# Second layer of a graph network: the running count of edges in one place of a PSUM bank, and a new order on VectorE

## The reference

```python
x = _layernorm(x + _L0_gnn_ref(x, node_vec, edge_weight, edge_attr_64, edge_index, ...))   # attention
x = _layernorm(x + _L1_gnn_ref(x, src, dst, edge_weight, W, b))

def _L1_gnn_ref(x, rows, cols, vals, W, b):        # rows = src, cols = dst
    gathered = vals[:, None] * x[cols]
    agg = jax.ops.segment_sum(gathered, rows, num_segments=N_NODES)
    return jnp.einsum('nc,oc->no', agg, W) + b
```

## Time and profile before

| what | value |
|---|---|
| median of 3 runs | 9,845.34 us (9,844.81 to 9,847.26) |
| profiled execution, its own time | 9,864.48 us |
| its span, first to last instruction | 9,862.8 us |
| mean granted PE clock over the span | 0.822 |
| busy share of the span | PE 77%, DVE 87%, ACT 52%, POOL 68% |
| second layer, first scan to end | 5,225.0 to 9,862.8 us |

### The profile page before, as it was taken

The page is one execution under the profiler, slowest core; times in us unless marked ns, Lnnn a source line. Parts: engine busy times, 40 slices in busy tenths (PEclk is TensorE's granted clock), DMA queues, the critical chain, the costliest instruction groups (busy, mean ns, idle before and its releaser), DMA issues.

```text
span 9862.8 us, 272152 instructions
## 1 busy us (share of the span) xinstructions
PE 7624.6 (77%) x52868; PEld 7101.3 (72%) x52869; DVE 8560.3 (87%) x21301; ACT 5115.0 (52%) x20838; POOL 6708.6 (68%) x6871
## 2 busy tenths in 40 slices
PE   6477777777777777777756777788888888888855
PEld 2477777777777777777756777787888877877754
DVE  5899999999999999999987666799999999999968
ACT  2377777777777777777753333333333333333300
POOL 0477777777777777777745777777777777777720
PEclk8688988888888888898875555688888888888888
DMA  6467666676666666666632222355555555555544
GB/s 191 114 180 178 179 177 177 178 179 178 176 177 180 177 176 177 178 181 177 177 97 69 71 71 71 106 151 147 149 147 149 148 148 149 148 148 149 148 133 116
DMA packets 1631706, 1484.67 MB, mean 151 GB/s; under 512 B 792007, under 2 KB 1363043, under 8 KB 1631203
## 3 DMA queue, kind: packets, MB, share of 16 engines
q1 hardware_dynamic: 1374244, 848.34, 34.3%
q0 software_dynamic: 257088, 632.95, 22.8%
HBM read 1225.51 MB, written 254.87 MB: 150 GB/s over the span
## 4 chain that ended last, share of the span: by engine, by line
issue 25%; DVE 19%; POOL 18%; PE 14%; DMA 7%; ACT 7%; DVEq 6%; SPq 3%; ACTq 2%; POOLq 0%
POOL message_scratch L869 17%; DMA message_scratch<-ohT,idx 6%; PE bank L982 3%; DVE y_all L1537 3%; PE bank L973 3%; ACT arena L1154 2%; DVEq L531 2%; PE bank L955 2%; PE bank L1015 2%; PE bank L963 2%; DVE acc L1670 1%; SPq L728 1%; DVE oh L1583 1%; DVE oh L1576 1%; DVE kve L1523 1%
## 5 line engine op out<-in xcount | busy, mean ns | idle before, releaser
L817 POOL DMA_INDIRECT kv<-kv_scratch,arena x3136 | 3265.7, 1041 | 1236.6 <-issue 837.5
L869 POOL DMA_INDIRECT message_scratch<-ohT,idx x3232 | 3214.2, 994 | 1079.0 <-issue 880.2
L1261 ACT ACTIVATE ohT<-bank,kv 128x128 f32<-128x128 f32 x3232 | 923.9, 369 | 2703.8 <-DMA message_scratch<-ohT,idx 2665.1
L1154 ACT ACTIVATE arena<-arena,weights 128x65 f32<-128x65 f32 x7040 | 1771.6, 337 | 2.4 <-PE bank L982 2.3
L1063 PE MATMUL bank<-acc,oh 128*128 x6464 | 1211.2, 345 | 520.3 <-ACT ohT L1262 514.4
L1063 PEld LDWEIGHTS bank<-acc,oh 128*128 128x128 f32 x6464 | 1054.7, 247 | 627.7 <-issue 625.2
L1077 PE MATMUL bank<-oh,kve 128*128 128x128 f32 x8640 | 1387.7, 321 | 144.7 <-DVE arena L1838 107.8
L982 PE MATMUL bank<-arena,oh 128*128 128x130 f32 x7040 | 1164.1, 318 | 280.8 <-DVE acc L1670 274.8
L1077 PEld LDWEIGHTS bank<-oh,kve 128*128 128x128 f32 x8640 | 1248.0, 227 | 167.8 <-issue 157.3
L982 PEld LDWEIGHTS bank<-arena,oh 128*128 128x128 f32 x7040 | 1048.2, 227 | 362.6 <-issue 295.1
L973 PE MATMUL bank<-arena,ohT 128*128 128x128 f32 x7040 | 1090.6, 306 | 0.0
(11 more groups left out here) (232 smaller groups left out, 12653.6 us busy)
## 6 DMA issues: line engine op xcount, KB each, us to landing
kve<-message_scratch SPq DMA_DIRECT2D x2160, 129.0 KB
kve<-nodes_scratch SPq DMA_DIRECT2D x880, 256.0 KB
feat<-in_edge_attr_dram SPq DMA_DIRECT2D x880, 96.0 KB
feat<-block_scratch SPq DMA_DIRECT2D x812, 98.0 KB
arena<-q_scratch SPq DMA_DIRECT2D x880, 64.0 KB
message_scratch<-ohT,idx POOLq DMA_INDIRECT x3232
kv<-kv_scratch,arena POOLq DMA_INDIRECT x3136
feat<-in_edge_attr_dram SPq DMA_DIRECT2D x880, 32.0 KB
```

Source lines behind the costliest of these rows:

```text
L817: pool.indirect_dma_start(kv[:, k, g, :], None, kv_d, bass.IndirectOffsetOnAxis(ap=group_rows[:, half, k * G + g, 0:1].bitcast(I32), axis= ...
L869: pool.indirect_dma_start(msg_d, bass.IndirectOffsetOnAxis(ap=idx[:, k, g:g + 1], axis=0), sum_ring[:, k % RING1, g, :], None).then_inc(s_ ...
L1154: op = act.activation(wv[:, st.k % 2, g, h, :], vR[:, st.k, g, h, :], ACT.Copy, scale=weights[:, st.k // ROUND, g, st.k % ROUND, h:h + 1])
L1261: act.activation(sum_ring[:, st.k % RING1, g, 0:C], banks[2 + st.k % 2][:, g * P:(g + 1) * P], ACT.Copy, scale=taken[:, st.k, g, 2:3])
```

## The change

The ranks move from two buffers in SBUF to one place in bank 0, 98 partitions of 512 numbers. The scan of a step then overwrites the ranks of the step before, so the product of the step before (found_stage) must come first: it moves from behind the row numbers to ahead of the first segment addition, and the scan waits for it. The carry and the scan move behind the first segment addition and the row numbers, and the copy of ranks (posw_stage) behind the scan.

```diff
--- before.py
+++ after.py
@@ -234,7 +234,6 @@
         seg_oh = oh_all[:, RING1 * G * P:RING1 * G * P + SEG_OH * SEGMENT * 2 * P].rearrange("p (h b a n) -> p h b a n", h=SEG_OH, b=SEGMENT, a=2)
         assert MT == 4 * SEGMENT and UNROLL1 % (MT // SEGMENT) == 0
         blk_row = feat_flat[:, RING1 * 2 * P:RING1 * 2 * P + KS * G * P // 2].bitcast(BF16).rearrange("p (k e) -> p k e", k=KS)
-        ranks = prod
         found1 = [featT_all[:, 0, :], featT_all[:, 1, :], feat_flat[:, 0:G * P], feat_flat[:, G * P:2 * G * P]]
         zeros = oh_all[:, QS * G * P * 2 - (CHUNK * NCHUNKS - COLS) * 4:QS * G * P * 2]
         W7 = FB * C
@@ -303,6 +302,7 @@
         featT_ps = banks[1][0:TD + MSG, :]
         e_ps, q_ps = banks[2:4], banks[4:6]
         agg_ps = [banks[6 + j][:, 0:HEADS * HB] for j in range(2)]
+        ranks = banks[0][0:NB, :]
         irow_ps, one_ps = banks[7][:, 0:P], banks[7][0:NB, P:P + 1]
         RANKS = SEGMENT * P
         mT_ps, small_ps = banks[0][:, 0:G * ROWS], banks[0][:, 128:128 + 4 * ROWS]
@@ -1754,26 +1754,26 @@
 
                 if st.k == 0 and not (isinstance(st.i, int) and st.i == 0):
                     dve.wait_ge(s_carry, st.s + st.i - 1)
-                    dve.tensor_tensor(carry[0:NB, :], ranks[0:NB, 1, G * P - 1:G * P], jump[0:NB, bass.ds(st.i, 1)], ALU.add).then_inc(s_carry, 1)
+                    dve.tensor_tensor(carry[0:NB, :], ranks[:, G * P - 1:G * P], jump[0:NB, bass.ds(st.i, 1)], ALU.add).then_inc(s_carry, 1)
 
             def count_stage(st):
 
                 dve.wait_ge(s_inblk, st.s + 1)
-                wait(dve, s_pos, st.before(2))
+                wait(dve, s_pos, st.s)
                 first = isinstance(st.i, int) and st.i == 0
                 if st.k == 0:
                     since = jump[0:NB, 0:1] if first else carry[0:NB, :]
                 else:
-                    since = ranks[0:NB, (st.k + 1) % 2, G * P - 1:G * P]
+                    since = ranks[:, G * P - 1:G * P]
                 wait(dve, s_carry, st.s + st.i)
-                dve.tensor_tensor_scan(ranks[0:NB, st.k % 2, :], one_ps.to_broadcast([NB, G * P]), in_blk[0:NB, st.k % 2, :], since,
+                dve.tensor_tensor_scan(ranks, one_ps.to_broadcast([NB, G * P]), in_blk[0:NB, st.k % 2, :], since,
                                        ALU.mult, ALU.add).then_inc(s_carry, 1)
 
             def found_stage(st):
 
                 dve.wait_ge(s_carry, st.s + st.i + 1)
                 wait(dve, s_rank, st.before(4))
-                dve.tensor_tensor(found1[st.k % 4][0:NB, :], ranks[0:NB, st.k % 2, :], in_blk[0:NB, st.k % 2, :], ALU.mult).then_inc(s_pos, 1)
+                dve.tensor_tensor(found1[st.k % 4][0:NB, :], ranks, in_blk[0:NB, st.k % 2, :], ALU.mult).then_inc(s_pos, 1)
 
             def posw_stage(st):
 
@@ -1845,11 +1845,11 @@
                     if own:
                         seg_blocks(i, k)
                     if pairs:
-                        at1(i, k, (onehot1_stage, 2), (carry_stage, 9), (count_stage, 9))
+                        at1(i, k, (onehot1_stage, 2), (found_stage, 8))
                     if segs:
                         seg(i, k, 0, 0, pairs, seg_add)
                     if pairs:
-                        at1(i, k, (posw_stage, 6), (place_stage, 0), (found_stage, 8))
+                        at1(i, k, (place_stage, 0), (carry_stage, 9), (count_stage, 9), (posw_stage, 6))
                     if segs:
                         seg(i, k, 1, 0, pairs, seg_add)
                     if pairs:
```

## The result

The changed kernel takes 9,755.6 us (median of 6 runs, 9,749.6 to 9,760.6) against 9,848.5 us (6 runs): 0.9903 of the time before, 95% interval 0.9891 to 0.9916, or 93 us less. Forecast were 9,751 us and -93.5 us. The profiled execution has a span of 9,752.1 us.

A forecast was written before the change was run, and what follows sets the result against it. POOL's scatters were taken to bound the second layer: 4,198.6 - 98 + 3, start +1.5, the 414 us behind unchanged, so -93.5 us; from the median 9,845.3 this gives 9,751 us. Range 9,736 to 9,795 us, some 0.8.

The forecast's parts named there:

- POOL is the bound and the excess sits in the scatters under the product: Second layer: everything waits for POOL; scatters exceed their median by 105 us, 100 us of it under L1776.
- The bank removes the delay: Product L1776, reading ranks from a bank, stops delaying scatters: 98 us off POOL's time, bounds 0 and 105.
- The order is worth nothing (price 0): Second layer's loop: the scan's wait and the copy of ranks 1.3 us later cost nothing; price 0.
- Scan 1,280 ns, product -10 ns: DVE, each step: scan from 1,274 to 1,280 ns (bounds 1,200 and 1,340), product 10 ns shorter (bounds -20 and 0).
- DVE can just follow, 3 us charged: Steps with segments: DVE keeps POOL's pace with 0.01 to 0.02 us a step to spare; 3 us charged for clustered waits.
- Waits of DVE for ACT under 20 us: Stretch with segments: DVE's waits for ACT fall from 68 us to under 20, a sign of the forecast.
- Start +1.5 us: Between first scans and first scatter: the scan's wait for the product adds 1 to 2 us, taken as 1.5.
- The rival of a dear scan: Steps with segments: a scan writing its bank and starting from it is dear; at +0.37 us, 9,953 us; chance 0.08.
- The rule of the Trainium skill: Product against scatters: two SBUF inputs contend with GpSimd, giving 98 us; or tensor_tensor leaves DMA descriptors alone, giving 0.

The follow-up runs named there:

- the pair of extra products: The changed kernel plus an unused product in steps without segments, both inputs in SBUF or one in a bank; 12,946.0 us (0.9891) and 12,963.3 us (0.9896).
- order_only_2: The changed kernel with its new order, but the one place of ranks in SBUF instead of the bank; 9,815.3 us against 9,847.3, 0.9967.
- Before_plus: The kernel before with one more small copy (128 x 32 from a bank) on DVE in each of 600 steps with pairs and segments; 12,882.3 us, 1.0008.

## Why the prediction was right, point by point

- *POOL is the bound and the excess sits in the scatters under the product.* Right. The excess fell from 105 to 4 us. With the 8 us of new idle time that makes -93 us, and the medians differ by 93. The profiled executions differ by more, 9,864.5 to 9,753.8 us: 13 us of it are the 4 ns by which the usual scatter was longer in the one before (962 against 958), about 4 us lie ahead of the first scatter. The prediction put the excess of one execution on the median without such a correction, and came out right since the excess does not contain this part.
- *The bank removes the delay.* Right as a mechanism: no scatter under L1776 exceeds 1.0 us in the changed kernel (some 450 such starts before, 348 of them over 1.0). The size attributed to it was wrong. Given the new order the bank is worth 74 - 4 = 70 us of excess, not 98.
- *The order is worth nothing (price 0).* This step failed. Alone it brings 32 us (21 to 45), 31 by the trace, all with segments, since products then start where they delay little. The two errors cancel in the sum, since the bank takes what the order leaves: the total was right, its division into parts was not. Also the copy of ranks came not 1.3 us later in the iteration: the product had moved ahead with it, and against the head of the iteration it is 0.6 us.
- *Scan 1,280 ns, product -10 ns.* 1,296 and -3 ns (684 to 681), inside the bounds. Together +19 ns a step where -4 was taken.
- *DVE can just follow, 3 us charged.* Nearly: 8 us of idle time of POOL. The margin of 0.01 to 0.02 us a step has been used up, by the scan and by L1751, which was not seen coming (+0.09 us a step with segments). DVE's row numbers were 20 us ahead of the scatters at step 200; this lead falls to 9 us at step 240 and to 2 to 4 us from step 400 on. In the kernel before it stays at 16 to 19 us from step 300 on, with the order alone at 12 to 15.
- *Waits of DVE for ACT under 20 us.* Right: none is left with segments.
- *Start +1.5 us.* The first scatter starts 4.3 us earlier, but 3.6 of these lie ahead of the first scan (5,221.4 for 5,225.0), where nothing was changed. What is left, 0.7 us less instead of 1.5 more, is below what executions differ by.
- *The rival of a dear scan.* It did not come. A slip in its sum changes nothing: 600 x 0.24 - 34 is 110, not 108.
- *The rule of the Trainium skill.* Of the two statements in "SBUF — State Buffer", Who interferes with whom, the one on two SBUF inputs is borne out by 1.37 us against 0.96 us in the pair of extra products; the one by which tensor_tensor leaves descriptors alone does not hold for these indirect scatters.

## What to carry to other kernels

Where GpSimd sets the pace, compare the mean of its instructions with their median, and look at what VectorE runs when the long ones start. A large operation of VectorE with both inputs in SBUF may then be worth moving to one with an input in PSUM, even if it gets no faster itself, as this product of 98 x 512 was; its place in the order decides how often it hurts. Undo each part of a change by itself before a gain is put down to one of them, and look first whether the comparison runs with the same bound.

## What the runs showed of the hardware

A VectorE product of 98 x 512 with two SBUF inputs that is under way when an indirect scatter begins, with over 0.13 us left, lets it end 0.83 us after the product, up to 1.53 us instead of 0.96; with one input in a bank nothing is added. If the two start within about 0.02 us of each other, the scatter takes its 0.96 us and the product up to 0.75 instead of 0.68. It works the other way too: a bf16 comparison of 98 x 512 takes 0.35 us alone and up to 0.59 us when begun with 0.50 to 0.26 us of a scatter left; begun with more than that left, it takes 0.35 us. A scan that writes a bank in place and takes its start from it costs 1,296 ns against 1,274 to 1,282 into SBUF. One and the same program, the kernel before, took 9.85 ms beside order_only_2 and 12.88 to 13.10 ms on three other chips; whether it is the chip was not tried. Before_plus, at 12.88 ms, has an unchanged tail and 1,032 us of idle time of PE without a named cause before matmuls of L1077, where the kernel before at 9.86 ms has 158.
